# Even load of Q and K, reordered GpSimd, V tiles between projection tiles, norm in two halves, 18 groups of scores ahead of the loop

## The chip, the cores and the metric

One core of a Trainium2 chip runs the whole kernel. The metric is device time in microseconds, the median of the runs. Engine names: PE is TensorE, DVE VectorE, ACT ScalarE, POOL GpSimd, SP SyncE, which issues DMAs.

## The reference

Eight batches of 1024 tokens with 256 features go through one block: a layer norm, then two branches whose sum is added to the input. Branch one is sliding-window attention (16 heads of 16 features, blocks of 64 queries, each against three blocks of keys with a band) with output projection, residual, norm, a gelu MLP of 1024, residual, norm. Branch two sends each token through one of eight experts, chosen by the largest score.

```python
x = L0_attn_x
xn = _layernorm(x, axis=-1)
x = x + attn_block(xn, ...) + expert_block(xn, gate_w, expert_w)

# attn_block
q, k, v = (x @ Wq + bq), (x @ Wk + bk), (x @ Wv + bv)      # by block of W = 64 and head
scores = einsum('bnqhd,bnkhd->bhnqk', q, kc) * scale       # kc: three blocks of keys
scores = where(band & valid, scores, -1e9)
out = einsum('bhnqk,bnkhd->bnqhd', softmax(scores), vc)
a = out @ Wo + bo
h = layer_norm(a + x, g1, b1)
f = gelu(h @ W1 + c1) @ W2 + c2
return layer_norm(f + h, g2, b2)

# expert_block
chosen = argmax(einsum('bsh,eh->bse', x, gate_w))
return x + (x @ expert_w[chosen].T)
```

## The kernel before

Tokens lie in T = 8 tiles of 128; the heads form G = 4 groups of four. The kernel is software-pipelined over the batches: `turn(b)` exists once for each engine, and the engines meet only at semaphores (`Count` objects; `x.at(b, k)` is the k-th event of batch b). Each engine runs its own list strictly in the order of the code. A turn has four stages.

**The loop**, `for k in range(STEPS + LAG)`, STEPS = 32 (group g, tile t). TensorE makes the transposed scores of step k (`scores_t`), ScalarE their exponentials (`exps`), GpSimd cuts the band in two passes (`band`, L468 and L473; in steps 22 to 27, `SHARED`, VectorE has the second pass), and TensorE multiplies with V (`values`) two steps later. A softmax needs each row's maximum first: `scores` (L1208) makes the scores once more in the other layout, in the two banks `SB`, one for each parity of the heads, VectorE reduces them (`maxima`, L739), and after a group's eight tiles `max_cols` (L1223) transposes the maxima, again into `SB`; they go through DRAM (`max_rows_out`, `max_rows_in`) into a row of `q_s`. The scores run LEAD = 14 steps ahead of the transposed ones: 14 groups are made before the loop, 18 in it. Beside this the loop does the next batch's norm (`c1_tile`, `c1_stage`, GpSimd's `rstd` at step 8, `xn_tile` in steps 10 to 13), its transposes (steps 14 to 17) and its Q and K (`qk_third`, two thirds of a tile in each of steps 18 to 29). SyncE takes Q and K through DRAM (`pair_stores`, `stack_loads`).

**b_stage**: for each tile a transpose of the heads' outputs (L1287), `normalize`, a transpose (L1295), the product with Wo (L1303) in two banks, and `b_sum` with statistics for the norm. Then come `c2_stage`, V and gate scores of the next batch, and the norm: variance (L789), GpSimd's `rstd` (L409), `nm1_stage` (L793), ScalarE's `n1_tiles` (L946), four transposes.

**d_stage, first half**: sixteen units of W1 (`w1_unit`, six matmuls of 512 columns in two banks `TB`), gelu (L1031) and its split into high and low halves (L995, L820), with the next batch's routing (`one_hot`, `ranks`, `routing_...`) and six groups of scores after units 5, 7 to 15.

**d_stage, second half**: for each of eight tiles `w2_tile` (24 matmuls), the next batch's sorted tokens through their expert (two tiles of 15 each time: `sorted_transposes` L1148, `xs_high`, `xs_low` L736, `sorted_expert`, `y_out`), one group of scores, `f_stats` (L798) and `f_out`. VectorE waits before all of it for `h_rdy` and `res_y`, both from GpSimd (L837, L839).

GpSimd's list in a turn sets much of the order:

```python
for k in range(STEPS):
    band(b, k)                      # rstd of the next batch after k == T
residual(b + 1)                     # L480, L483
rstd(b, 1, ve1, rs1)
residual_attn(b + 1)                # L489
fetch(b, last)                      # gathers L521, then the add L527
send(b + 1)                         # scatters L507
residual_mlp(b)                     # L496, L499
for t in range(T): rstd(b, 2, ve2, rs2, t)
```

`fetch` waits until `store_res(b + 1)` has landed, since it writes into `x_sb`. `load_x` reads the batch after the next into `x_sb` late in the sorted tiles, and `send` scatters `xn` by expert.

## Time and profile before

| | us |
|---|---|
| median of 3 runs | 1473.32 |
| lowest and highest | 1461.51, 1473.76 |
| the profiled execution | 1471.13 |
| its span, first to last instruction | 1469.3 |
| PE busy in the span | 1200.0 (82%) |
| DVE, POOL, ACT busy | 924.3, 825.5, 726.5 |
| mean granted TensorE clock | 0.928 |

Matmuls are pipelined and their modelled ends overlap, so a busy PE is not PE at its peak; starts are the better measure. The page's chain of waits is followed back from the last instruction, at each step to what released it. In a timeline a row can merge several instructions of one line; the bracket at its end tells how long the engine was idle before it and what ended that.

### The profile page before, as it was taken

The numbers are of one execution on the slowest core, as the hardware profiler recorded it, in microseconds if no ns is written. First come the engines' busy times: TensorE is split into PE (matmuls) and PEld (weight loads), VectorE is DVE, ScalarE is ACT, GpSimd is POOL, SyncE is SP. The second block draws the span as 40 slices with busy tenths as digits, with TensorE's granted clock in tenths as the row PEclk, the third lists the DMA queues.
The fourth block names the chain that finished last, engine by engine and source line by source line (L and its number), as shares of the span: only waits on it lengthen the run. The fifth ranks groups of instructions, "written<-read, shape, count | busy, mean of one in ns | idle before, by whom it ended". The sixth has DMA issues, their size and how long they took to land.

```text
span 1469.3 us, 32444 instructions
## 1 busy us (share of the span) xinstructions
PE 1200.0 (82%) x11720; PEld 726.1 (49%) x11720; DVE 924.3 (63%) x2207; ACT 726.5 (49%) x1355; POOL 825.5 (56%) x1088
## 2 busy tenths in 40 slices
PE   0717898799879898898987898798986989878877
PEld 0414454554637445464545546374454645365445
DVE  8554657476656746776575766577474765656455
ACT  1304657146562574436572575526763365725661
POOL 6551568435781567625674457815676266834664
PEclk9958999899989899999998999898998999999989
DMA  8443081231723254230812327231532408122010
GB/s 250 120 130 116 31 199 50 80 127 44 163 76 104 73 132 99 72 125 31 199 51 80 126 59 156 69 109 67 147 85 72 124 32 202 54 85 87 3 29 29
DMA packets 93977, 142.89 MB, mean 97 GB/s; under 512 B 10592, under 2 KB 62688, under 8 KB 91744
## 3 DMA queue, kind: packets, MB, share of 16 engines
q1 hardware_dynamic: 87680, 124.04, 30.6%
q0 software_dynamic: 6144, 16.79, 3.6%
q8 instruction: 100, 1.64, 0.5%
q14 instruction: 53, 0.43, 0.1%
HBM read 74.47 MB, written 68.29 MB: 97 GB/s over the span
## 4 chain that ended last, share of the span: by engine, by line
PE 42%; POOL 26%; issue 12%; DVE 7%; ACT 3%; DMA 3%; another core or an unknown queue 0%; DVEq 0%; POOLq 0%; SPq 0%; ACTq 0%
PE bank L1180 6%; PE bank L1268 5%; PE bank L1078 5%; PE bank L1081 5%; PE bank L1079 5%; PE bank L1173 4%; POOL x_sb L521 4%; DVE m_sb L745 4%; POOL xs_dram L507 4%; POOL res_r L527 3%; POOL pool L496 3%; POOL pool L499 3%; POOL x_sb L483 3%; POOL x_sb L480 3%; PE bank L1148 2%
## 5 line engine op out<-in xcount | busy, mean ns | idle before, releaser
L981 ACT ACTIVATE pool<-bank 128x512 f32<-128x512 f32 x512 | 285.5, 596 | 150.9 <-PE bank L1180 147.5
L745 DVE TENSOR_REDUCE m_sb<-bank 128x2 f32<-128x384 f32 x512 | 261.5, 552 | 130.3 <-PE bank L1188 128.7
L468 POOL TENSOR_SCALAR_AFFINE_SELECT pool<-pool 128x512 f32<-128x512 f32 x256 | 183.6, 717 | 244.1 <-ACT pool L981 205.5
L1180 PE MATMUL bank<-q_s,k_s 128*128 128x256 f16 x1024 | 185.1, 289 | 15.7 <-ACT pool L981 8.8
L412 POOL TENSOR_TENSOR rs<-ve,neghalf 128x1 f32<-128x1 f32 x64 | 36.9, 577 | 251.7 <-DVE ve L806 251.7
L1268 PE MATMUL bank<-pool,v_a 128*32 128x256 f32 (+2 forms) x2560 | 166.7, 352 | 8.4 <-POOL pool L473 8.3
L970 ACT ACTIVATE xn<-bank 128x256 f32<-128x256 f32 x120 | 46.0, 384 | 224.4 <-PE bank L1081 218.6
L1173 PE MATMUL bank<-k_s,q_s 48*64 48x192 f16 x2048 | 99.1, 270 | 58.9 <-DVE m_sb L745 40.5
L1180 PEld LDWEIGHTS bank<-q_s,k_s 128*128 128x128 f16 x1024 | 82.5, 101 | 126.3 <-issue 97.4
L820 DVE TENSOR_TENSOR pool<-pool 128x512 f16<-128x512 f32 x128 | 105.5, 827 | 62.1 <-ACT pool L995 52.7
L473 POOL TENSOR_SCALAR_AFFINE_SELECT pool<-pool 128x512 f32<-128x512 f32 x208 | 133.4, 641 | 0.0
L1078 PE MATMUL bank<-w_h,pool 128*128 128x256 f16 x512 | 126.0, 288 | 0.5 <-DVE pool L798 0.5
L1079 PE MATMUL bank<-w_l,pool 128*128 128x256 f16 x512 | 125.6, 288 | 0.0
L1031 ACT ACTIVATE pool<-bank,c1c 128x512 f32<-128x512 f32 x128 | 87.7, 685 | 48.9 <-PE bank L1081 33.3
L1173 PEld LDWEIGHTS bank<-k_s,q_s 48*64 48x64 f16 x2048 | 42.4, 109 | 134.5 <-issue 134.5
L1078 PE MATMUL bank<-tr_h,w_h 128*128 128x512 f16 x256 | 98.9, 386 | 4.6 <-ACT pool L1031 4.4
L736 DVE TENSOR_TENSOR pool<-bank,pool 128x256 f16<-128x256 f32 x120 | 46.0, 417 | 85.8 <-POOL pool L499 61.9
L1079 PE MATMUL bank<-tr_l,w_h 128*128 128x512 f16 x256 | 98.5, 385 | 0.0
L1148 PE MATMUL bank<-ident,xn 128*128 128x128 f32 x240 | 46.8, 310 | 62.6 <-DMA xn<-xs_dram 59.7
L1268 PEld LDWEIGHTS bank<-pool,v_a 128*32 128x32 f32 x2560 | 53.5, 111 | 84.2 <-issue 45.4
L962 ACT ACTIVATE pool<-bank 128x256 f16<-128x256 f32 x120 | 41.3, 382 | 89.3 <-PE bank L1148 87.7
L995 ACT ACTIVATE pool<-pool 128x512 f16<-128x512 f32 x128 | 80.6, 630 | 4.1
(154 smaller groups left out, 2644.6 us busy)
## 6 DMA issues: line engine op xcount, KB each, us to landing
pair_dram<-pool SPq DMA_DIRECT2D x96, 256.0 KB, 4.2
xn<-xs_dram SPq DMA_DIRECT2D x40, 384.0 KB, 3.6
ys_dram<-xn SPq DMA_DIRECT2D x120, 128.0 KB, 1.8
q_s<-pair_dram SPq DMA_DIRECT2D x32, 384.0 KB, 6.7
k_s<-pair_dram SPq DMA_DIRECT2D x32, 384.0 KB, 8.3
x_sb<-in_L_attn_x SPq DMA_DIRECT2D x8, 1024.0 KB, 5.8
res_dram<-x_sb SPq DMA_DIRECT2D x8, 1024.0 KB, 5.2
res_r<-res_dram SPq DMA_DIRECT2D x8, 1024.0 KB, 5.0
```

The source lines that it names most:

```text
L468: nc.gpsimd.affine_select(out=p, in_=p, compare_op=ALU.is_ge, fill=0.0, base=0, pattern=[[0, 4], [1, 2 * W]], channel_multiplier=-1).then_ ...
L473: nc.gpsimd.affine_select(out=p, in_=p, compare_op=ALU.is_ge, fill=0.0, base=0, pattern=[[0, 4], [-1, 2 * W]], channel_multiplier=1).then_ ...
L745: nc.vector.tensor_reduce(m_sb[:, 4 * g + par:4 * g + 4:2, t], SB[par][:, 0:2 * WIN].rearrange("p (h c) -> p h c", h=2), AX.X, ALU.max).th ...
L820: nc.vector.tensor_tensor(gL[hf][:, c, :], g32[:, u % 2, :], gH[hf][:, c, :], ALU.subtract).then_inc(g_lo.sem, 1)
L981: nc.scalar.activation(prob[:, (k + 2) % 3, par::2, :], TB[par][:, :].rearrange("p (h q) -> p h q", h=2), ACT.Exp, scale=EXP_SCALE).then_i ...
L995: nc.scalar.activation(gH[hf][:, c, :], g32[:, u % 2, :], ACT.Copy).then_inc(g_hi.sem, 1)
L1031: nc.scalar.activation(g32[:, u % 2, :], TB[u % 2][:, :], ACT.Gelu_apprx_tanh, bias=c1c[:, c:c + 1], scale=1.0 / WS).then_inc(gel.sem, 1)
L1078: nc.tensor.matmul(dst, lh[c], rh[c], start=start and c == 0, stop=False)
L1079: nc.tensor.matmul(dst, lh[c], rl[c], start=False, stop=False)
L1173: return nc.tensor.matmul(out[W * n:W * n + W, i * WIN:i * WIN + WIN], q_s[r, 2 * h + par, q:q + W], k_s[r, h, q - W:q + 2 * W], start=i = ...
L1180: return nc.tensor.matmul(out[:, i * QW:i * QW + QW], k_s[:, h, W + t * P:W + t * P + P], q_s[:, 2 * h + par, t * P:t * P + QW], start=Tru ...
L1268: mm = nc.tensor.matmul(OB[hf][32 * hl:32 * hl + 32, a - hf * HALF:z - hf * HALF], v_a[:, t, 4 * g + hl, :], prob[:, (k + 2) % 3, hl, q0:q ...
```

## The change

- Loop: LEAD is 18, so 14 groups of scores are made in the loop (steps 1 to 14), one bank (parity) at a time between the transposed scores (`scores_half`). `xn_tile` moves to steps 2 to 5, the transposes to 6 to 9, Q and K are spread over steps 12 to 31 at 24 thirds in 20 steps (`thirds_at`). `max_cols` uses other banks (`XB`), for groups 0 and 1 in d_stage, 2 at step 10, 3 at step 16, and waits only for its own group's maxima.
- The next batch's `c1_tile` and `c1_stage` move from the loop to the second half of d_stage of the turn before, `load_x` from sorted tile 10 to tile 2; GpSimd's `rstd` for it stands ahead of the first `band`.
- GpSimd: the sixteen residual adds go between the bands of steps 6 to 21; the gathers go ahead of the second norm's root, which is made in two halves; the add of what was gathered is a step of its own (`add_fetched`). SyncE's `store_res` goes ahead of the last two stack loads.
- b_stage: V tiles of the next batch are made between the projection tiles, in the banks `SB`. `n1_stats`, `rstd_half`, `n1_shift` and `n1_tiles` work on four tiles each.
- d_stage: two more groups of scores, ahead of unit 0 and of unit 1, then one after each odd unit: ten ahead of the second half, eight in it. `one_hot` goes to b_stage, `ranks` behind unit 0, with the last two transposes of the norm.

The diff, cut to its core (SyncE, GpSimd, VectorE, ScalarE, TensorE in this order):

```diff
-LEAD = 14
-MAX_AT = 4
+LEAD = 18
+MAX_AT = {10: 2, 16: 3}
...
-    XN_AT = T + 2
...
-    QK_AT = XT_AT + 4
...
+    QK_AT = T + 4
+    RES_AT = XN_AT + 4
...
+    W1_STEPS = range(1, 2 * FC, 2)
+    assert 2 + len(W1_STEPS) + T == LEAD
...
+    def thirds_at(k):
+
+        n = STEPS - QK_AT
+        return range(max(0, k - QK_AT) * 24 // n, max(0, k + 1 - QK_AT) * 24 // n) if k < STEPS else range(0)
...
-        QB, VB = MB, OB + TB
+        QB, VB = MB, SB
+
+        XB = [MB[0], MB[1], MB[0], SB[1]]
...
-                    if i == 6:
+                    if i == 3:
                         max_rows_out(b, 0)
-                    if i == 8:
+                    if i == 5:
                         max_rows_in(b, 0)
-                    if i == 10 and x_next:
+                    if i == 2 and x_next:
                         load_x(b + 1)
...
+                    store_res(b + 1)
                     for i in range(2, 4):
                         stack_loads(b + 1, i)
-                    store_res(b + 1)
                     sorted_tiles(b + 1, x_next)
                 store_out(b)
...
+                if not last:
+                    rstd(b + 1, 0, ve0, rs0)
                 for k in range(STEPS):
                     band(b, k)
-                    if k == T and not last:
-                        rstd(b + 1, 0, ve0, rs0)
-                if not last:
-                    residual(b + 1)
-                rstd(b, 1, ve1, rs1)
+                    if RES_AT <= k < RES_AT + 2 * T and not last:
+                        residual_tile(b + 1, k - RES_AT)
+                fetch(b, last)
+                for hf in range(2):
+                    rstd_half(b, hf)
                 if not last:
                     residual_attn(b + 1)
-                fetch(b, last)
+                add_fetched(b)
                 if not last:
                     send(b + 1)
                 residual_mlp(b)
...
                         normalize(b, s)
+                        if not last:
+                            v_out(b + 1, s)
                     if s >= 4:
                         b_sum(b, s - 4)
-                dve.wait_ge(bn1.sem, bn1.at(b, T))
-                dve.sem_inc(passed, 1)
-                for t in range(T):
-                    nc.vector.bn_aggr(mv[:, 1, t, :], st[:, 1, t, :]).then_inc(ag1.sem, 1)
...
-                                               op0=ALU.mult, op1=ALU.mult).then_inc(nm1.sem, 1)
+                    if s == T - 1:
+                        n1_stats(b, 0)
+                n1_stats(b, 1)
+                n1_shift(b, 0)
+                if not last:
+                    one_hot(b + 1)
+                n1_shift(b, 1)
...
-                for u in range(0 if last else 2, 4):
+                for u in range(2):
                     n1_low(b, u)
                 if not last:
-                    one_hot(b + 1)
+                    maxima(b + 1, 0)
+                    routing_tiles(b + 1)
+                for u in range(2, 4):
+                    n1_low(b, u)
+                if not last:
+                    routing_positions(b + 1)
+                    maxima(b + 1, 1)
                 for u in range(2 * FC):
                     gelu_low(b, u)
                     if u == 0 and not last:
-                        routing_tiles(b + 1)
-                    if u == 1 and not last:
-                        routing_positions(b + 1)
-                    if u == 2 and not last:
                         routing_experts(b + 1)
                     if u in W1_STEPS and not last:
-                        maxima(b + 1, W1_STEPS.index(u))
+                        maxima(b + 1, 2 + W1_STEPS.index(u))
                 dve.wait_ge(res_y.sem, res_y.at(b, T))
...
                     if not last:
-                        if t == 3:
-                            max_cols(b + 1, 0)
+                        if t in (1, 7):
+                            max_cols(b + 1, t // 7)
                         maxima(b + 1, LEAD - T + t)
                     f_out(b, t)
+                    if t >= TH and b < NB - 2:
+                        for i in range(2 * (t - TH), 2 * (t - TH) + 2):
+                            c1_tile(b + 2, i)
                 if not last:
                     keep_positions(b + 1)
+                if b < NB - 2:
+                    c1_stage(b + 2)
...
+                        max_cols(b, MAX_AT[k])
                     if 1 <= k and k - 1 + LEAD < STEPS:
...
-                for u in range(4):
-                    hf, c = divmod(u, DC)
-                    act.wait_ge(nT_ps.sem, nT_ps.at(b, u + 1))
-                    nc.scalar.activation(tr_h[:, c, hf * HALF:hf * HALF + HALF], MB[u % 2][:, :], ACT.Copy).then_inc(nT_h.sem, 1)
+                n1_tiles(b, 0)
+                for u in range(2):
+                    n1_high(b, u)
+                n1_tiles(b, 1)
                 for u in range(2 * FC):
+                    if u == 1:
+                        for i in range(2, 4):
+                            n1_high(b, i)
                     c = u % FC
...
-                nc.tensor.transpose(SB[g % 2][0:4 * T, 0:P], m_sb[:, 4 * g:4 * g + 4, :].rearrange("p h t -> p (h t)"),
+            def scores_half(b, j, par):
+
+                scores_wait(b, j, par)
+                for i in range(2):
+                    for n in range(2):
+                        score_mm(SB[par], n, j, par, i)
+                for n in range(2):
+                    mm = mask_mm(SB[par], n, j % T, par)
+                mm.then_inc(S_ps.sem, 1)
+
+            def max_cols(b, g):
+                pe.wait_ge(mx.sem, mx.at(b, 2 * T * (g + 1)))
+                if g == 2 and b < NB - 1:
+                    pe.wait_ge(xT_l.sem, xT_l.at(b + 1, 3))
+                nc.tensor.transpose(XB[g][0:4 * T, 0:P], m_sb[:, 4 * g:4 * g + 4, :].rearrange("p h t -> p (h t)"),
                                     ident[:, :]).then_inc(mT_ps.sem, 1)
 
...
             def b_stage(b, last):
+                if not last:
+                    v_tile(b + 1, 0)
                 for s in range(T + 4):
                     if s < T:
...
                         mm.then_inc(t1_ps.sem, 1)
+                        if t + 1 < T and not last:
...
                     n1_transposes(b, u, last)
+                if not last:
+                    scores(b + 1, 0)
                 for u in range(2 * FC):
                     w1_unit(b, u, last)
-                    if u == 1 and not last:
-                        ranks(b + 1)
+                    if u == 0:
+                        if not last:
+                            ranks(b + 1)
+                        for i in range(2, 4):
+                            n1_transposes(b, i, last)
...
+                        if not last:
+                            scores(b + 1, 1)
                     if u in W1_STEPS and not last:
-                        scores(b + 1, W1_STEPS.index(u))
+                        scores(b + 1, 2 + W1_STEPS.index(u))
...
                 for k in range(STEPS + LAG):
-                    if k % T == MAX_AT and k < 3 * T:
-                        max_cols(b, k // T + 1, min(k - 1 + LEAD, STEPS))
+                    if k in MAX_AT:
+                        max_cols(b, MAX_AT[k])
                     for par in range(2):
                         if k < STEPS:
                             scores_t(b, k, par)
-                        if QK_AT <= k < QK_AT + 12 and not last:
-                            qk_third(b + 1, *divmod(2 * (k - QK_AT) + par, 3))
-                    if 1 <= k and k - 1 + LEAD < STEPS:
-                        scores(b, k - 1 + LEAD)
+                        if not last:
+                            for third in list(thirds_at(k))[par:par + 1]:
+                                qk_third(b + 1, *divmod(third, 3))
+                        if 1 <= k and k - 1 + LEAD < STEPS:
+                            scores_half(b, k - 1 + LEAD, 1 - par)
```

## Rows read from the trace of the kernel before

**Rows 1.** The page: chain of waits by engine; a DMA issue, with median us to landing
```profile
PE 42%; POOL 26%; issue 12%; DVE 7%; ACT 3%; DMA 3%; another core or an unknown queue 0%; DVEq 0%; POOLq 0%; SPq 0%; ACTq 0%
...
res_dram<-x_sb SPq DMA_DIRECT2D x8, 1024.0 KB, 5.2
```
**Rows 2.** Windows: start:end, length, busy us by engine, clock, DMA share, GB/s
```profile
481.10:549.20 68.10, 60.95 (x733) 28.62 (x734) 40.45 (x88) 47.21 (x85) 40.80 (x62) 0.92 0.36 101
549.20:564.20 15.00, 14.08 (x94) 11.96 (x93) 12.66 (x42) 3.61 (x9) 10.32 (x15) 1.00 0.84 204
...
614.00:651.90 37.90, 37.05 (x393) 30.31 (x390) 28.15 (x76) 10.41 (x30) 4.64 (x9) 1.00 0.33 106
```
**Rows 3.** Timeline, GpSimd, 548 to 615: start, us, engine, line, operation
```profile
548.44 5.53 POOL L480 TENSOR_TENSOR x_sb<-x_sb,xn 128x256 f32<-128x256 f32 x8
...
564.31 1.65 POOL L409 TENSOR_TENSOR rs<-ve,neghalf 128x8 f32<-128x8 f32 x1 [4.72 <-DVE ve L789]
...
571.61 1.06 POOL L521 DMA_INDIRECT x_sb<-ys_dram,pos_y  x1 [0.16 <-issue]
...
583.39 7.41 POOL L527 TENSOR_TENSOR res_r<-res_r,x_sb 128x256 f32<-128x256 f32 x8 [1.90 <-DMA x_sb<-ys_dram,pos_y]
...
607.23 7.18 POOL L499 TENSOR_TENSOR pool<-pool,bc 128x256 f32<-128x256 f32 x8
```
**Rows 4.** Waits: who waited for whom, us in total, times, longest
```profile
DVE pool L736 <- POOL pool L499: 61.9, 7, 12.4
```
**Rows 5.** Timeline, TensorE: first matmuls of two V tiles
```profile
562.71 0.29 PE L1078 MATMUL bank<-wvg_h,tr_h 128*128 128x264 f16 x1 [0.52 <-DVE pool L772]
...
563.39 0.28 PE L1078 MATMUL bank<-wvg_h,tr_h 128*128 128x264 f16 x1
```
**Rows 6.** Timeline, VectorE: a V tile's evacuation, and one step's maxima
```profile
564.14 0.42 DVE L666 SCALAR_TENSOR_TENSOR v_a<-bank,bc 128x256 f32<-128x256 f32 x1
...
1362.15 1.02 DVE L745 TENSOR_REDUCE m_sb<-bank 128x2 f32<-128x384 f32 x2 [0.77 <-PE bank L1188]
```
**Rows 7.** Timeline, ScalarE: the norm's tiles and the load of gelu's table
```profile
566.72 4.04 ACT L946 ACTIVATE pool<-pool,nm,rs 128x256 f32<-128x256 f32 x8 [5.78 <-DVE nm L793]
...
574.76 1.28 ACT L1031 ACT_TABLE_LOAD   x1
```
**Rows 8.** Timeline, ScalarE: a stop in one turn; first and last gelu of another
```profile
582.95 0.69 ACT L1031 ACTIVATE pool<-bank,c1c 128x512 f32<-128x512 f32 x1 [4.31 <-remote]
...
916.92 0.69 ACT L1031 ACTIVATE pool<-bank,c1c 128x512 f32<-128x512 f32 x1
...
941.29 0.67 ACT L1031 ACTIVATE pool<-bank,c1c 128x512 f32<-128x512 f32 x1
```
**Rows 9.** Timeline, TensorE, one loop step with transposes (the next begins at 517.59)
```profile
515.49 0.61 PE L1180 MATMUL bank<-q_s,k_s 128*128 128x256 f16 x4
516.03 0.36 PE L1173 MATMUL bank<-k_s,q_s 48*64 48x192 f16 x8
...
516.44 0.66 PE L1087 MATMUL bank<-ident,xn 128*128 128x128 f32 x4
...
517.02 0.64 PE L1268 MATMUL bank<-pool,v_a 128*32 128x256 f32 x8
```
**Rows 10.** Timeline, TensorE, last turn: scores of two steps in a row
```profile
1361.53 0.36 PE L1173 MATMUL bank<-k_s,q_s 48*64 48x192 f16 x8 [0.21 <-DVE m_sb L745]
...
1363.32 0.36 PE L1173 MATMUL bank<-k_s,q_s 48*64 48x192 f16 x8 [0.20 <-DVE m_sb L745]
```
**Rows 11.** Timeline, TensorE: scores before and after a transpose of maxima
```profile
488.36 0.53 PE L1173 MATMUL bank<-k_s,q_s 48*64 48x192 f16 x8
...
491.35 0.36 PE L1173 MATMUL bank<-k_s,q_s 48*64 48x192 f16 x8
```
**Rows 12.** Timeline, last turn: GpSimd's last band pass, VectorE's first `f_stats`
```profile
1389.50 0.64 POOL L473 TENSOR_SCALAR_AFFINE_SELECT pool<-pool 128x512 f32<-128x512 f32 x1
...
1443.20 0.42 DVE L798 SCALAR_TENSOR_TENSOR pool<-bank,pool 128x256 f32<-128x256 f32 x1 [2.79 <-POOL pool L499]
```

185 lines of the change are left out of this document (94 added, 91 removed).

## The prediction

> **What bounds the kernel now.** I read the page first: its chain of waits says whether one engine sets the end. None does; TensorE has 42% of the chain, GpSimd 26%, and 12% is waiting that nothing explains [rows 1]. The windows of one turn of the batch loop, cut at the table loads that start the exponentials (481.1 and 651.9), show where to look: the turn takes 170.8 us, the attention loop 68.1 of them, the output projection 15.0 with TensorE busy for 14.1, and the second half of the feed-forward part 37.9 with TensorE busy for 37.05 [rows 2]. Only in the 50 us between, from 564 to 614, is TensorE loose. GpSimd's timeline says what runs there [rows 3]: the residual adds start when the loop ends (548.44) and end at 559.59 (564.31 less its 4.72 of waiting); then the reciprocal root; the bias add, 5.6 us; eight gathers from 571.61; the add of what they brought, 7.4 us to 590.8; eight scatters; two passes over `n1`, to 614.4. The scatters take 10.9: 607.23 less 590.8 less a first pass that I take at 5.5, like the equal residual pass. VectorE's waits close it: `xs_low` waited for L499, the last pass, in all seven turns, 61.9 us [rows 4]. So GpSimd's queue is the path from the loop's end (549.1) to 614.4, 65.3 us of each 170.8.
>
> **GpSimd's queue after the change.** Removed from it behind the loop are the 11.1 us of residual adds. Moved are the gathers, ahead of the root, so that they run beside the output projection; what is queued behind their waits is the root itself. They wait for `store_res`, which stands in SyncE's queue behind the pair stores of the last Q/K tile: 1 us after the loop's end plus 5.2 us to land [rows 1], in a crowded stretch, so I take 8 (bounds 4 and 15). With 11 us for issue and landing (571.61 to 583.39 less a 1.90 us wait is 9.9) they end 19 after the loop. Then two half roots, 1.0 each (estimate from 1.65 for all eight columns), 5.6, 7.4, 10.9 and 12.8: 56.7 us in place of 65.3. Alone this would be worth 8.6 us a turn.
>
> **The other path becomes the later one.** TensorE, ScalarE and VectorE have their own chain from the loop's end to the first `f_stats`.
> - Output projection. A V tile costs 0.68 us of TensorE (562.71 to 563.39) [rows 5]; eight are 5.4. They leave a stretch where they lay under the norm's chain for one where TensorE is full (14.1 of 15.0). Some 1 us fits into its first gaps, and half of the statistics are done early (0.4): 15.0 + 5.4 - 1.4 = 19.0. VectorE gets 8 x 0.42 [rows 6] on its 12.7: 16.1, just below. Bounds: 18 (gaps of 2) and 22 (the two engines in turn).
> - Norm. Four tiles 2.0 (half of 4.04), first transposes 0.9, two copies 1.1 (estimate, a little over a tile of 0.5 each), four tiles 2.0, table 1.3 [rows 7]: 7.4; and 0.8 for the shift, since the root stands behind the gathers. First gelu at 19.0 + 8.2 = 27.2 after the loop. Before it was 576.05 - 549.1 = 27.0: the V tiles eat what the halves give.
> - Sixteen gelus. First to last start took 24.4 us in a quiet turn; in another ScalarE stood for 4.31 us at an unknown queue and it was 33 [rows 8]. I take 27.0 for the mean. Two more groups of scores are in it, 0.55 each (0.40 of TensorE, 516.03 to 516.44 [rows 9], and a hand-over). VectorE's order at the start is new: two `n1_low`, maxima, five routing operations, two more `n1_low`, four more of routing, maxima, and only then `gelu_low(0)`, for which the third gelu waits. That is some 5.5 us (1.0 for each maxima [rows 6], 0.7 for a pass of 512 columns, 0.25 for the small ones, estimates) against 2.6 for two gelus: 3 us late, two copies of ScalarE hidden in it. 27.0 + 1.1 + 3.0 = 31.1; bounds 26 and 36.
> - Last gelu to first `f_stats`: 0.7, transposes 0.5, `w2_tile` 24 matmuls or four V tiles, 2.7: 3.9.
>
> That is 62.2 us after the loop. Before it was 614.4 and one pass of 0.4 for `xs_low`, so 65.7 to 66. GpSimd's 56.7 now ends before. Gain 3.7, bounds -1 and 8.
>
> **The loop.** A step with transposes takes 2.10 us, all TensorE's: 0.54 for the transposed scores, 0.40 for scores and masks, 0.59 for transposes, the rest 0.57 for values [rows 9]. A plain step has 1.51 of such work but takes 1.79 (1361.53 to 1363.32), for both score banks are filled together and VectorE must empty them before the next [rows 10]. One bank at a time takes that wait away, but the score matmuls then run two abreast and not four. The 0.40 us now hold four streams of 640 columns. Two abreast, each half costs those 640 columns (0.27 us at 2.4 GHz) and about 0.1 for the change of tile shape (516.03 less 515.49 less 4 x 0.107): 0.75 a step. Bounds: 0.53, no cost for the change, and 1.17, nothing abreast. I take 0.75, as the interval with four abreast holds that same 0.1.
> The Trainium skill, TensorEngine Tiling (Array Packing), Key Properties, says that changing the tiling mode drains the engine; the row agrees, with some 0.1 us. The change goes from three such changes in a scoring step to five, so by that rule the halves are not free; by a free change of mode a step would cost 0.2 less.
>
> Step by step after: 2.5 to the first band and 1.2, as now; step 1 2.4; 2 to 5 VectorE's, maxima 1.02 and two tiles of `xn`, 2.1; 6 to 9 1.86 + 0.59 = 2.45; 10 and 11 2.0; 12 to 14 with a third of a Q/K tile (0.43) 2.3; 15 to 21 GpSimd's, two bands of 0.62 and one residual tile 0.69 [rows 3, 12], 1.93; 22 to 30 0.57 + 0.54 + 1.2 x 0.43 = 1.65; 1.8 from the last band to the last values. Sum 65.4. The transposes of the maxima are in it at nothing: three of them stopped the scores for 1.2 us each, 2.99 from 488.36 to 491.35 in place of 1.79 [rows 11]; now they use the banks of the `xn` transposes and scores long finished, and if they collide there it costs 0.3 each. The root for the next batch now stands ahead of the first band, behind `c1_stage` at the end of VectorE's turn: 0.6 late. So 66.0 for 68.0: 2.0 gained, bounds -4 (halves at 1.17) and 6.
>
> **The second half.** TensorE sets it (37.05 of 37.9 [rows 2]). The stop for the maxima's transpose goes there too, 0.8 (like the 1.2 in the loop, less for the tile beside it). Eight `bn_stats` of 0.42, a pass of 256 columns as in [rows 6], go into the last four tiles, 0.84 each, where VectorE, busy for 28.15 of the 37.9, has 1.2 idle in each, half of it usable. I take 1.2 lost: 0.4 worse, bounds -0.8 and 3. `load_x` in the middle of the sorted loads: 0.6, bounds 0 and 2.
>
> **The sum.** 3.7 + 2.0 - 0.4 - 0.6 = 4.7 us a turn, seven turns: 33. The last turn has no V, no Q/K and no scatters: its loop loses four scoring steps and two stops, 3.6, and its first `f_stats` comes at 48 in place of 53 us after the loop (1443.2 less the last band's end, 1390.1 [rows 12]), 5.2. The prologue gains four groups of scores, beside GpSimd's sends, and 4 us of statistics partly in the way: 2.5 lost. 33 + 8.8 - 2.5 = 39.3. The profiled execution took 1471.1: 1431.8, and the median of the runs shown is 2.2 above it: 1434.
>
> **The rivals.**
> 1. *As forecast*, the gate moves from GpSimd to the chain through the gelus, 2.5 to 7 us a turn: 1418 to 1452. Chance 0.52.
> 2. *More*: VectorE keeps pace at the start of the gelus (26 to 28 us in all) and the halves cost 0.53: 4 us more a turn: 1385 to 1418. For it speaks that TensorE has slack there, against it the fixed order. Chance 0.24.
> 3. *Taken back in the loop*: halves at 1.17, 14 x 0.42 = 5.9 us a turn less than forecast: 1434 + 41 = 1475; 1460 to 1478. Against it: L1268 runs its column groups abreast in one bank, eight matmuls of 256 columns in 0.57 [rows 9]. Chance 0.11.
> 4. *It does not do what it says*: the gathers get free only 15 us after the loop, the queue ends at 64, and nothing is gained there: 1455 to 1470. Chance 0.04.
> 5. *Slower*: stops of ScalarE for an unknown queue [rows 8]. Before, they lay ahead of GpSimd's gate and cost nothing; now each one counts. The place is between the first and the last gelu; at 37 us in each turn (6 more than I take) the time is 1476, and it decides from 39: 1490. One turn had 33 with two groups fewer. Chance 0.09.
>
> **How the numbers follow.** The runs shown differ by 0.8%, so about 1% can be told: below 1458.6 is faster, above 1488 slower. Faster: 1 and 2, 0.76. Same: 3 and 4, 0.15. Slower: 0.09. Range: from 1405, which cuts a third of case 2, to 1466, within cases 3 and 4.
>
> **What would show it.** Right: no wait of `xs_low` for L499; the gathers inside an output projection of 19 us; scoring steps of 1.9 us; no stop at the maxima's transposes. Wrong: an output projection above 22 us, first to last gelu above 34, a loop above 68.

## The result, and the profile after

The kernel after takes 1557.18 us (median of 4 runs, 1546.97 to 1590.88), the one before 1473.54 in the same session: ratio 1.055, interval 1.047 to 1.063. It is slower by 5.5%, and the forecast was 1434. Ratios with an interval, here and below, are of the executions in the faster of two states that every kernel shows; where "no interval" is said, too few were in it, and the ratio is the rougher one of the medians of all. The profiled execution has a span of 1555.6 us, 123.8 more than the 1431.8 of the forecast's sum.

The page of the kernel after: span, granted clock of TensorE in 40 slices (tenths of full speed), chain of waits by engine, and the group of the gathers (busy, mean ns | idle before it, and what ended it).

```profile
span 1555.6 us, 32461 instructions
...
PEclk9957699979898598977989699995889889896799
...
PE 68%; DVE 14%; issue 7%; ACT 5%; DMA 3%; POOL 2%; SPq 0%; DVEq 0%; POOLq 0%; ACTq 0%
...
L541 POOL DMA_INDIRECT x_sb<-ys_dram,pos_y x64 | 61.4, 960 | 77.7 <-DMA res_dram<-x_sb 60.5
```

GpSimd's share of the chain fell from 26% [rows 1] to 2%: the gate has moved, as forecast. But TensorE's went from 42% to 68%. The windows of the turn that begins at 494.4 say where (columns as in [rows 2]: PE, PEld, DVE, ACT, POOL busy, clock, DMA share, GB/s).

```profile
494.40:499.40 5.00, 3.44 (x28) 1.62 (x28) 4.42 (x18) 4.13 (x6) 1.12 (x1) 0.80 0.51 176
499.40:529.40 30.00, 29.64 (x214) 12.14 (x216) 15.58 (x28) 11.35 (x20) 14.73 (x24) 0.50 0.15 51
529.40:549.40 20.00, 20.00 (x188) 8.16 (x180) 8.11 (x15) 11.38 (x20) 13.13 (x22) 0.78 0.01 3
549.40:577.00 27.60, 24.87 (x262) 11.44 (x261) 11.71 (x13) 21.96 (x41) 20.74 (x31) 1.00 0.61 144
577.00:598.60 21.60, 18.36 (x128) 15.24 (x126) 15.79 (x60) 3.69 (x10) 8.77 (x10) 1.00 0.89 208
```

The loop takes 82.6 us here (494.4 to 577.0) against 68.1 before [rows 2]. For 30 us TensorE is busy 29.64 us by the trace, whose ends of matmuls are modelled, and is granted 0.50, that is 1.2 GHz. The output projection, 21.6, runs at full clock. In the timeline of TensorE one scoring step at 1.2 GHz looks like this (start, us, line; L1222 transposed scores, L1215 and L1230 a half's scores and masks, L1129 transposes of `xn`, L1319 values):

```profile
521.24 0.61 PE L1222 MATMUL bank<-q_s,k_s 128*128 128x256 f16 x2
521.77 0.53 PE L1215 MATMUL bank<-k_s,q_s 48*64 48x192 f16 x4
522.10 0.42 PE L1230 MATMUL bank<-mask,ident 64*64 64x256 bf16 x2
522.45 0.61 PE L1222 MATMUL bank<-q_s,k_s 128*128 128x256 f16 x2
522.99 0.53 PE L1215 MATMUL bank<-k_s,q_s 48*64 48x192 f16 x4
523.31 0.42 PE L1230 MATMUL bank<-mask,ident 64*64 64x256 bf16 x2
523.66 1.11 PE L1129 MATMUL bank<-ident,xn 128*128 128x128 f32 x4
524.70 1.08 PE L1319 MATMUL bank<-pool,v_a 128*32 128x256 f32 x8
525.72 0.61 PE L1222 MATMUL bank<-q_s,k_s 128*128 128x256 f16 x2
```

The step is 4.48 us long (521.24 to 525.72) against 2.10 before [rows 9], and nothing in it waits: no row has an idle time. From start to start transposes and values have almost doubled, 1.04 for 0.58 and 1.02 for 0.57; the transposed scores with the halves take 2.42 for 0.95. What changed is the clock.

The turns of the kernel after differ among themselves, and their loops are the longer the lower the clock was. These are the whole loops of the turns from 1046.0 and from 320.7, the longest and the shortest of the seven full ones:

```profile
1046.00:1130.50 84.50, 80.40 (x687) 33.95 (x684) 39.85 (x73) 48.75 (x85) 49.57 (x75) 0.72 0.28 77
320.70:393.10 72.40, 68.73 (x683) 30.53 (x684) 39.72 (x73) 48.74 (x84) 49.71 (x75) 0.86 0.34 89
```

The code is the same in both, and so are the busy times of VectorE, ScalarE and GpSimd (columns three to five).

Stages, means over the seven full turns, read from the timelines as distances between first and last instructions (for the kernel before the same reading). "Loop" runs from the table load of the exponentials to the last values, "first to last gelu" from the first one's start to the last one's end (the forecast's 31.1 was from start to start; 0.7 for the last gelu is added here and taken from its 3.9 behind):

| us | before | forecast | after |
|---|---|---|---|
| loop | 68.3 | 66.0 | 79.3 (72.4 to 84.5) |
| loop of the last turn | 56.3 | 52.7 | 73.6 |
| output projection | 14.8 | 19.0 | 21.3 |
| loop's end to first gelu | 26.1 | 27.2 | 29.7 |
| first to last gelu | 27.1 | 31.8 | 31.3 (28.7 to 35.0) |
| loop's end to first `f_stats` | 65.1 | 62.2 | 64.2 |
| first `f_stats` to the turn's end | | 38.3 | 38.0 |

Against the forecast: 7 x 13.3 = 93 us in the loops of the full turns, 73.6 - 52.7 = 21 in the last one, 7 x 2.0 = 14 between loop and `f_stats`. That is 128, less 1 in the last turn and 2 in the second halves: 125 for the 124 us of the miss. Nine tenths of it are in the loop.

### The profile page after: what moved, and what is told of

Its sections match the earlier page's. It is cut to its first block, busy times and chain, and to the rows that moved or that the text cites. A ratio compares the mean times of both kernels' runs of the same rounds, so it can differ in the third digit from the quotient of the medians.

```text
span 1555.6 us, 32461 instructions
## 1 busy us (share of the span) xinstructions
PE 1349.9 (87%) x11720; PEld 764.7 (49%) x11720; DVE 975.9 (63%) x2223; ACT 741.3 (48%) x1355; POOL 817.1 (53%) x1096
## 3 DMA queue, kind: packets, MB, share of 16 engines
q8 instruction: 100, 1.64, 0.4%
## 4 chain that ended last, share of the span: by engine, by line
PE 68%; DVE 14%; issue 7%; ACT 5%; DMA 3%; POOL 2%; SPq 0%; DVEq 0%; POOLq 0%; ACTq 0%
PE bank L1222 10%; PE bank L1319 10%; PE bank L1120 9%; PE bank L1121 8%; PE bank L1123 8%; PE bank L1215 7%; PE bank L1129 3%; PE bank L1230 3%; DMA ys_dram<-xn 2%; PE bank L1190 2%; DVE st L634 2%; PE bank L1358 2%; DVE xn L663 2%; PE bank L1154 2%; DVE pool L775 2%
## 5 line engine op out<-in xcount | busy, mean ns | idle before, releaser
L1022 ACT ACTIVATE pool<-bank 128x512 f32<-128x512 f32 x512 | 299.7, 599 | 214.6 <-PE bank L1222 210.5
L1222 PE MATMUL bank<-q_s,k_s 128*128 128x256 f16 x1024 | 230.8, 316 | 12.7 <-ACT pool L1022 8.8
L1215 PE MATMUL bank<-k_s,q_s 48*64 48x192 f16 x2048 | 161.5, 297 | 55.9 <-DVE m_sb L763 45.2
L1319 PE MATMUL bank<-pool,v_a 128*32 128x256 f32 (+2 forms) x2560 | 187.5, 391 | 18.3 <-POOL pool L486 9.8
L1222 PEld LDWEIGHTS bank<-q_s,k_s 128*128 128x128 f16 x1024 | 74.1, 102 | 174.2 <-issue 143.1
L1215 PEld LDWEIGHTS bank<-k_s,q_s 48*64 48x64 f16 x2048 | 60.6, 117 | 185.2 <-issue 185.2
L852 DVE TENSOR_TENSOR pool<-pool 128x512 f16<-128x512 f32 x128 | 117.7, 922 | 47.0 <-ACT pool L1036 45.9
L1230 PE MATMUL bank<-mask,ident 64*64 64x256 bf16 x1024 | 129.1, 329 | 0.0
L682 DVE SCALAR_TENSOR_TENSOR pool<-bank,bqk,pool 128x512 f16<-128x512 f32 x64 | 47.9, 749 | 113.8 <-ACT pool L998 112.8
L1120 PE MATMUL bank<-w_h,pool 128*128 128x256 f16 x512 | 115.3, 273 | 0.0
L1319 PEld LDWEIGHTS bank<-pool,v_a 128*32 128x32 f32 x2560 | 58.9, 119 | 94.2 <-issue 42.4
L541 POOL DMA_INDIRECT x_sb<-ys_dram,pos_y x64 | 61.4, 960 | 77.7 <-DMA res_dram<-x_sb 60.5
```

What stands on the lines that cost most here:

```text
L852: nc.vector.tensor_tensor(gL[hf][:, c, :], g32[:, u % 2, :], gH[hf][:, c, :], ALU.subtract).then_inc(g_lo.sem, 1)
L1022: nc.scalar.activation(prob[:, (k + 2) % 3, par::2, :], TB[par][:, :].rearrange("p (h q) -> p h q", h=2), ACT.Exp, scale=EXP_SCALE).then_i ...
L1120: nc.tensor.matmul(dst, lh[c], rh[c], start=start and c == 0, stop=False)
L1215: return nc.tensor.matmul(out[W * n:W * n + W, i * WIN:i * WIN + WIN], q_s[r, 2 * h + par, q:q + W], k_s[r, h, q - W:q + 2 * W], start=i = ...
L1222: return nc.tensor.matmul(out[:, i * QW:i * QW + QW], k_s[:, h, W + t * P:W + t * P + P], q_s[:, 2 * h + par, t * P:t * P + QW], start=Tru ...
L1230: return nc.tensor.matmul(dst, ident16[r, :], band, start=False, stop=True, skip_group_check=True)
```

## The experiments

Kernels sent together ran on one chip, one after the other, beside the kernel before; ratios are to that. There were five such groups, A to E. Why they have to be kept apart comes out in C and D.

| group | before, us | kernels |
|---|---|---|
| A | 1480.07 | a_full, b_half, a_adj, a_twice |
| B | 1483.84 | a_v1, a_late_fetch, a_between, n_latev |
| C | 1475.88 | a_warm, a_cold, n_shift, n_split |
| D | 1486.38 | after_2, a_adj_2, a_warm_2, n_early |
| E | 1471.03 | n_shift_2, n_safe |

### Is it the halved scores?

**a_full**: scores four abreast again, behind both transposed scores; all else of the change stays.

```diff
-                        if 1 <= k and k - 1 + LEAD < STEPS:
-                            scores_half(b, k - 1 + LEAD, 1 - par)
+                    if 1 <= k and k - 1 + LEAD < STEPS:
+                        scores(b, k - 1 + LEAD)
```

> The changed kernel with one thing undone: in the loop's 14 scoring steps both parities of a group are made together, four score matmuls abreast, behind the two transposed scores, as before the change. Theory CLOCK (the score matmuls two abreast keep TensorE at its lower level of 1.2 GHz until the scores are done): granted clock back to 0.92 or more, loop 66 to 69 us instead of 72 to 85, 1435 to 1455 us in all. Rival PLACE (the low clock comes from what the change put into the loop's first steps, norm, transposes, and the later start of Q and K): the loop stays above 76 us and the time above 1500.

Measured: 1468.61 us, ratio 0.993 (0.989 to 0.996), mean clock 0.94 against 0.87; loop 62.6. The clock came back as the theory said, the loop was shorter than its 66 to 69, and the time, outside its 1435 to 1455, was longer for another reason (the section on 1466 and 1436). One edit of the change carries the loss: 6% against the 1.055 of the kernel after, 7 to 10% against its repeat in group D (1575.90 to 1622.06 us there).

**b_half**: the other side. The kernel before, with only its scores halved and interleaved in the same way (the diff above reversed, with `scores_half` added).

> The kernel before with this one part of the change: scores made one parity at a time, each behind its transposed score, in the 18 scoring steps of the loop. Theory CLOCK: granted clock near 0.85, steps of 3.4 us at the lower level, loop 80 us or more, 1560 to 1620 us. Rival PLACE: the halves cost only their work at full clock, 0.75 for 0.40 us of which the old wait for VectorE hides most: 1480 to 1500 us.

Measured: 1668.09 us, ratio 1.120 (1.111 to 1.129), mean clock 0.81, full turns' loops of 82 to 96 us. The halves alone do it, and without the rest of the change they do it worse than the expected 1560 to 1620. The shortest of these loops, from 926.6, is worth a look:

```profile
928.60:952.50 23.90, 22.05 (x278) 9.76 (x280) 18.08 (x48) 14.93 (x26) 16.27 (x25) 1.00 0.26 89
952.50:983.00 30.50, 30.43 (x207) 12.38 (x208) 12.45 (x22) 11.90 (x21) 8.57 (x14) 0.50 0.01 2
```

Here the first eleven steps with halves ran at full clock. The clock fell at 952.5, after TensorE had waited 0.91 and 0.45 us around a transpose of maxima, and stayed at 0.50 until the scoring steps were over.

**a_adj**: still two halves, each with its own wait and bank, but one behind the other, after both transposed scores.

```diff
-                        if 1 <= k and k - 1 + LEAD < STEPS:
-                            scores_half(b, k - 1 + LEAD, 1 - par)
+                    if 1 <= k and k - 1 + LEAD < STEPS:
+                        scores_half(b, k - 1 + LEAD, 1)
+                        scores_half(b, k - 1 + LEAD, 0)
```

> The changed kernel, with the two halves of a group one right behind the other, behind both transposed scores: still two abreast, but changes of tile shape as few as before the change. Theory CLOCK by streams abreast: nothing is cured, 1530 to 1560 us, scoring steps of 3.2 to 3.4 us at 1.2 GHz. Rival SHAPES (it is the alternation of transposed scores and halves that holds the clock down): 1440 to 1470 us.

Measured: 1466.28 us, ratio 0.993 (0.989 to 0.997), loop 62.8, clock 0.94. The halves may stay, if they are adjacent, and the expectation named for that case is the one met. My theory, that two streams abreast in place of four keep the clock down, does not fall with it, though the expectation said so: as the step below shows, adjacent halves overlap and do run four abreast. Its windows for the turn from 482.2, and one of its steps with transposes:

```profile
487.20:492.20 5.00, 3.80 (x38) 1.37 (x38) 3.19 (x7) 1.08 (x2) 4.71 (x8) 0.51 0.33 96
492.20:517.20 25.00, 25.00 (x346) 13.13 (x342) 17.92 (x37) 18.44 (x34) 21.25 (x35) 0.96 0.11 43
```

```profile
500.84 0.61 PE L1222 MATMUL bank<-q_s,k_s 128*128 128x256 f16 x4
501.38 0.37 PE L1215 MATMUL bank<-k_s,q_s 48*64 48x192 f16 x8
501.57 0.29 PE L1230 MATMUL bank<-mask,ident 64*64 64x256 bf16 x4
501.80 0.66 PE L1129 MATMUL bank<-ident,xn 128*128 128x128 f32 x4
502.38 0.64 PE L1319 MATMUL bank<-pool,v_a 128*32 128x256 f32 x8
502.95 0.61 PE L1222 MATMUL bank<-q_s,k_s 128*128 128x256 f16 x4
```

The clock falls to 0.51 at the loop's start in this kernel too, and comes back within the next window; in the kernel after it stays down for 30 us. The step takes 2.11 us. The two adjacent halves take 0.42 together (501.38 to 501.80), as four abreast did [rows 9]: issued back to back they lie on different rows of the array and overlap. Set apart, they take 0.39 each even at full clock: in the kernel after, one runs from 543.16 to the next transposed score at 543.56, 0.40.

```profile
543.16 0.35 PE L1215 MATMUL bank<-k_s,q_s 48*64 48x192 f16 x4
543.35 0.28 PE L1230 MATMUL bank<-mask,ident 64*64 64x256 bf16 x2
543.56 0.39 PE L1222 MATMUL bank<-q_s,k_s 128*128 128x256 f16 x2
```

**a_between**: whole scores, but between the two transposed scores of a step: four changes of tile shape in a step, where the kernel after has five and a_adj three.

```diff
-                        if 1 <= k and k - 1 + LEAD < STEPS:
-                            scores_half(b, k - 1 + LEAD, 1 - par)
+                        if par == 0 and 1 <= k and k - 1 + LEAD < STEPS:
+                            scores(b, k - 1 + LEAD)
```

> The kernel after with its scores four abreast again but placed whole between the two transposed scores of a step: TensorE changes between full-array and quarter-array tiles four times in a scoring step, against five with the halves interleaved and three with the scores behind both transposed scores. If the cost is in the number of changes, the loop falls between the two: 63 us with three changes, 72 to 84 with five, so 66 to 74, and the total about 1480 to 1530. If what counts is that a score lies between the two transposed scores at all, it is as slow as the kernel after, 1540 to 1570. If it is the halves alone, it is as the version with whole scores behind, 1465 to 1472.

Measured: 1478.45 us, ratio 1.000 (0.996 to 1.004), loop 64.2 (63.6 to 65.1), clock 0.94, below the 66 to 74 and the 1480 that were expected of four changes. One more change of shape costs 1.4 us a loop and leaves the clock alone. The kernel after, 15 us more, differs from it in two things at once: five changes for four, and score matmuls that run two abreast and not four. No run has one without the other, so which of the two holds the clock down is not shown. What is shown is that halves set apart by a full-array matmul do it, and whole scores or adjacent halves do not.

**a_twice**: the kernel after with each transposed score of the scoring steps made twice, the same result written again. It adds only work.

```diff
-                for i in range(2):
-                    mm = score_t_mm(TB[par], k, par, i)
+                for r in range(2 if 1 <= k <= STEPS - LEAD else 1):
+                    for i in range(2):
+                        mm = score_t_mm(TB[par], k, par, i)
```

> The changed kernel with work added: in the 14 scoring steps each transposed score is made twice, the second time over the first with the same values, four more matmuls of the full array a step. At 1.2 GHz that is 0.85 us more a step, at 2.4 GHz 0.43. Theory CLOCK, if what counts is how much of the array's work there is: the clock rises earlier, and the kernel gets faster by the added work, 1470 to 1530 us. If the added matmuls do not bring the clock up: 14 x 8 x 0.85 = 95 us slower, 1640 to 1660 us.

Measured: 1538.16 us, ratio 1.046 (1.037 to 1.055; the kernel after 1.047 to 1.063), mean clock 0.95, loop 71.7; 1470 to 1530 was expected. It has 14 x 4 matmuls of 256 columns more in a turn, 6 us at the 0.107 of the forecast, and its loop is 7.6 us shorter than that of the kernel after (79.3; 81.0 in group D). Its clock hardly falls: in four of the seven full loops not at all, in the others for 3 to 7 us. One without a fall, from 502.4:

```profile
502.40:517.40 15.00, 12.69 (x148) 6.85 (x148) 12.37 (x34) 8.29 (x13) 8.45 (x12) 1.00 0.45 156
517.40:537.40 20.00, 20.00 (x227) 10.79 (x225) 11.55 (x21) 11.62 (x20) 12.97 (x22) 1.00 0.01 3
```

More work in the loop, less time for it: the loss is in the clock and not in the work. In a_twice interleaved halves do not hold the clock down.

### Does interleaving pull the clock down, or does it keep it from coming back?

**a_warm**: adjacent halves in the first seven scoring steps (k 1 to 7), interleaved ones in the other seven (k 8 to 14). **a_cold**: the reverse.

```diff
 # a_warm
-                        if 1 <= k and k - 1 + LEAD < STEPS:
+                        if 8 <= k and k - 1 + LEAD < STEPS:
                             scores_half(b, k - 1 + LEAD, 1 - par)
+                    if 1 <= k < 8:
+                        for par in range(2):
+                            scores_half(b, k - 1 + LEAD, 1 - par)
```

> The kernel after with its half scores adjacent, behind both transposed scores, in the first seven scoring steps of a turn (k from 1 to 7), and interleaved as in the kernel after in the other seven (k from 8 to 14). In every kernel so far the granted clock falls to about 0.5 in the first 10 us of the loop; with adjacent halves it is 1.00 again 10 to 15 us after the loop began, with interleaved ones it stays at 0.50 for 35 us with TensorE busy throughout. If interleaving only hinders the clock's return once it is down, it is up by step 8 and stays up: the loop takes 62 to 65 us and the kernel 1460 to 1480 us. If interleaving takes the clock down by itself, the granted clock falls to 0.5 to 0.7 from step 8 on, at about 20 us into the loop, and the kernel takes 1500 to 1530 us.

> The reverse: interleaved halves in k from 1 to 7, adjacent ones from 8 to 14. If interleaving hinders the clock's return, the clock stays at 0.5 until step 8, at 27 to 30 us into the loop (7 steps of 3.4 us), and comes back within a few steps of it, so the loop takes about 7 x 1.5 = 10 us more than with adjacent halves: 70 to 74 us, the kernel 1510 to 1540. If it takes the clock down by itself in later steps only, the kernel is near 1466 us.

Measured: a_warm 1436.55 us, ratio 0.976 (0.969 to 0.984), loop 65.9; a_cold 1486.74, ratio 1.008 (1.003 to 1.012), loop 71.0. The loops are 0.9 above and within what the theory of the return gave (62 to 65 and 70 to 74); both times are 23 us below its ranges, which were reckoned from a_adj's 1466 and so held something that this group does not have (next section). Windows of a_warm (turn from 471.4), then of a_cold (turn from 483.4):

```profile
476.40:481.40 5.00, 3.89 (x40) 1.44 (x37) 3.01 (x7) 1.30 (x3) 4.71 (x8) 0.50 0.38 100
481.40:491.40 10.00, 10.00 (x136) 5.05 (x134) 8.23 (x18) 6.52 (x12) 6.63 (x12) 0.85 0.25 101
491.40:496.40 5.00, 5.00 (x58) 2.52 (x57) 3.66 (x8) 3.42 (x6) 3.96 (x7) 1.00 0.01 2
496.40:511.40 15.00, 15.00 (x175) 6.85 (x177) 7.40 (x14) 10.61 (x19) 12.72 (x21) 1.00 0.01 3
```

```profile
488.40:508.40 20.00, 19.16 (x149) 7.58 (x148) 11.29 (x21) 7.35 (x13) 9.86 (x17) 0.50 0.22 76
508.40:513.40 5.00, 5.00 (x41) 2.41 (x41) 2.27 (x4) 2.57 (x5) 3.10 (x6) 0.60 0.01 2
513.40:528.40 15.00, 15.00 (x204) 7.57 (x203) 8.64 (x17) 11.73 (x22) 13.89 (x24) 1.00 0.01 3
```

In a_warm the interleaved steps begin at 496 and run at 1.00, here and in all its turns. In a_cold's turn the clock stays at 0.50 as long as the steps are interleaved; the first adjacent one begins at 510.25 and the next, at 513.29, is at full speed. So interleaving does not take the clock down; once it is down, it delays its return. How long is not fixed. In two of a_cold's seven full turns the clock was back during the last interleaved step, and in the kernel after it comes back with the steps still interleaved in all seven: in steps 7 to 9 in three turns, in step 12 in three, in step 14 in one, after 20 to 48 us. From step 6 on transposes of the full array join, from step 12 on matmuls of Q and K. In the turn of the windows the return falls on the first of these (two matmuls of 512 columns, then a half at full speed):

```profile
537.25 0.63 PE L1154 MATMUL bank<-tr_h,wqk_h 128*128 128x512 f16 x1
...
538.24 0.39 PE L1215 MATMUL bank<-k_s,q_s 48*64 48x192 f16 x4
```

In a_twice, too, more full-array work stands beside the halves. Whether that or the order decides, the runs do not separate.

A fall near the head of the loop occurs in every version, though not in every turn, in the kernel before too (0.57 and 0.74 in its windows from 483.3 to 493.3), and what goes before it is TensorE's waiting there: 3.44 us busy in the first 5 of the kernel after.

a_warm is the kernel after but for seven steps of each turn, and measured 1436.6 where 1434 was forecast. Its other stages are those of the kernel after: projection 21.4, loop's end to `f_stats` 62.6. This close a figure is luck in part: its seven adjacent steps save 2.6 us a turn (group D), 18 in all, which the forecast kernel would not have.

### Why adjacent halves gave 1466 and not 1436

In group A the loop of a_adj was 62.8 us, shorter than forecast, and still the gain was 0.7%. The loss was behind the loop: projection 26.1, first `f_stats` 69.4 after the loop's end, forecast 19.0 and 62.2. Five runs asked what is in that.

**a_v1**: a_adj with only the first of the six matmuls of each V tile of batches 1 to 7 (the V rows and gates of those batches are therefore others, and the routing with them).

```diff
-                mm = triple(VB[t % 2][:, 0:D + E], ...)
+                mm = nc.tensor.matmul(VB[t % 2][:, 0:D + E], tr_h[:, 0, s], wvg_h[:, 0], start=True, stop=True)
```

> The kernel after with its two half scores adjacent, and of each V tile of batches 1 to 7 only the first of its six matmuls of width 400 made (the other five left out, so V and the gates of those batches are not the reference's). The question is the output projection, which took 25.6 us from the end of the loop to the first V eviction in the parent, where the prediction had 19. If the matmuls of V are what lengthens it, 8 x 5 fewer matmuls at 0.17 to 0.33 us each give 7 to 13 us per turn less of TensorE's work, and the stretch falls to about 16 to 20 us; the time falls by 7 turns x 6 to 9 us, from 1466 to about 1400 to 1425 us. If it is the chain through the extra tile's eviction and semaphores, or the stops that the trace lays on an unknown queue, the stretch stays at 23 to 26 us and the time above 1450.

Measured: 1451.38 us, ratio 0.980 (0.972 to 0.988); projection 23.4. Forty matmuls fewer gave 2.7 us (across groups A and B). They have 264 columns, not the 400 of the expectation, so what was left out is 5/6 of 8 x 0.68 [rows 5], 4.5 us and not 7 to 13: the matmuls are a part of it, the stops or the evictions the rest.

**a_late_fetch**: a_adj with the gathers back behind the roots and the bias add, out of the projection.

```diff
-                fetch(b, last)
                 for hf in range(2):
                     rstd_half(b, hf)
                 if not last:
                     residual_attn(b + 1)
+                fetch(b, last)
```

> The kernel after with adjacent halves and the row gathers put back behind the roots and the residual on GpSimd, so that no gather runs inside the output projection. If the gathers' traffic (DMA engines busy 0.78 in that stretch) is what stops VectorE and ScalarE there, the stretch falls from 25.6 to about 19 to 21 us, and the gathers then gate the feed-forward again: the first gelu at 35 us or later, total 1455 to 1475. If V's work is what lengthens it, the stretch stays at 24 to 26 us, and the total rises by the later gathers, to 1475 to 1500.

Measured: 1491.71 us, ratio 1.006 (1.003 to 1.009); projection 21.4, just above the 19 to 21 of the first theory, but first to last gelu 37.2 where a_adj had 31.8. The total was missed, since the lost time went along with the gathers: what had stopped the projection now stopped the gelus. After the loop's end a_adj issues its gathers at 7.9 to 17.7 us, and stops end at 16 to 20; here it is 28.3 to 38.4 and 35 to 40. A second set goes with GpSimd's scatters: issued at 39 to 51 us and stops ending at 45 to 53 in a_adj, 47 to 58 and 54 to 60 here.

What stopped them is marked in the timelines as ended by "remote", another core or an unknown queue. In the kernel after no such instruction exists, in a_warm and a_cold neither; a_adj, a_full, a_twice, a_v1, a_between and a_late_fetch have 29 to 40 of them, n_latev (below) 13, the kernel before 8, b_half 6. **after_2**, **a_adj_2** and **a_warm_2** are the kernel after, a_adj and a_warm again, together.

> The kernel after once more, beside the others of this call. Expected as before: the loop 72 to 85 us at a granted clock of 0.5 in its first 35 us, no stop that the trace lays on an unknown queue, 1545 to 1570 us.

> The kernel after with adjacent halves once more. In its first profile VectorE and ScalarE stood still together in each output projection for 2 to 5.6 us, ended by something of another core or an unknown queue, while the gathers ran; in the kernels of the last call, with the same projection and the same gathers beside it, no such stop is in any turn. If the stops come with the chip or the hour, they are absent here too, the projection takes 21.3 us instead of 25.6, and the time is about 4.3 x 7 = 30 us below 1466: 1430 to 1440 us. If they belong to this kernel's code, they are here again and the time is 1455 to 1475.

> The kernel with adjacent halves in its first seven scoring steps and interleaved ones behind, once more. If the stops come with the chip or the hour, it measures the same as the version with adjacent halves throughout, or up to 15 us more (its loop was 65.7 us against 62.8). If they belong to the other kernel's code, it is 25 to 35 us faster.

Measured in group D: after_2 1609.45 us (1575.90 to 1622.06; 1.083 of the kernel before by the medians, no interval), a_adj_2 1470.82, ratio 0.989 (0.985 to 0.993), a_warm_2 1500.82, ratio 1.009 (1.004 to 1.013). Projections 26.8, 26.8, 26.5. All three have the stops, a_warm_2 too, which had none in group C and 0.976. So whether there are any does not belong to the code: in A, B and D every kernel traced shows them, in C and E none. Nor does it belong to the chip: A and E ran on the same one. Where and how long they are does depend on the code: n_latev, in group B with the same early gathers but no V tiles there, has none in the projections of its seven full turns. After_2's expectation, no stops, was wrong.

Two of them in a_adj_2, ScalarE's row first, then VectorE's:

```profile
563.67 0.38 ACT L1057 ACTIVATE pool<-bank 128x256 f32<-128x256 f32 x1 [5.82 <-remote]
```

```profile
563.61 0.42 DVE L790 TENSOR_TENSOR pool<-bank,xnbo 128x256 f32<-128x256 f32 x1 [1.91 <-remote]
...
565.08 0.26 DVE L781 RECIPROCAL rec<-bank 128x16 f32<-128x16 f32 x1 [0.58 <-remote]
```

Both engines come back at the same moment, 563.6, in a stretch where the DMA engines are 0.74 busy, and TensorE's clock is 0.87 over the projection (its window in a_adj_2, then in a_warm of group C):

```profile
546.10:572.00 25.90, 21.04 (x125) 16.49 (x122) 14.55 (x51) 3.15 (x9) 8.75 (x9) 0.87 0.74 171
```

```profile
537.00:560.00 23.00, 19.58 (x148) 15.65 (x140) 16.13 (x57) 4.56 (x11) 9.94 (x11) 1.00 0.85 195
```

That they follow the gathers, and the scatters, is shown (a_late_fetch moved both). What they are is not. A candidate is the engines' own instructions arriving late: the page of the profile has a queue "q8 instruction" with 100 packets and 1.64 MB, the same in the runs without stops. The Trainium skill, Runtime: NRT & Kernel Launch, Instruction fetch mechanics, says that each engine's instructions are fetched by DMA in blocks of 16 KiB; the page of the profile agrees in size, 16.4 KB a packet. No run shows that these packets come late, nor why some groups have stops and others not.

Inside group D a_warm_2 is 2% slower than a_adj_2, with loops of 65.5 and 62.9. The loops are 18 us of the 30 between the medians; the traces, of executions of 1485.0 and 1468.89 us, do not show the rest. Seven interleaved steps at full clock cost 2.6 us, 0.37 each, which is the 2 x 0.39 of two halves apart less the 0.42 of two together.

### A version from the findings

**n_latev**: whole scores behind the transposed ones; V tiles out of the projection, four before the norm's first transposes, two behind them, two behind the first W1 unit; 16 groups of scores ahead in place of 18.

```diff
             def d_stage(b, last):
+                if not last:
+                    for t in range(TH):
+                        v_tile(b + 1, t)
                 for u in range(2):
                     n1_transposes(b, u, last)
-                if not last:
-                    scores(b + 1, 0)
+                if not last:
+                    for t in range(TH, TH + 2):
+                        v_tile(b + 1, t)
...
```

> A version of my own: scores whole and behind both transposed scores, V tiles taken out of the output projection and put around the norm's first transposes (four before, two behind, two after the first projection unit), sixteen groups of scores ahead, GpSimd's early gathers kept. If TensorE's work in the output projection is what the kernel after loses there, the projection returns to 15 to 17 us after the loop's end, the V tiles fill the wait for the norm, the first gelu comes at 27 to 30 us, and the time is 1396 to 1430. If the stops there are the gathers' traffic, the projection stays above 20 us and the time is 1440 to 1465.

Measured: 1457.20 us (1438.32 to 1466.52; 0.982 by the medians, no interval). The projection is at 15.0 again, as expected, the total was missed by 27 us at the median and by 8 at the lowest. In three turns the first gelu comes 7 us later than in the rest, and one row of VectorE says why, beside GpSimd's:

```profile
398.25 8.31 DVE L807 SCALAR_TENSOR_TENSOR nm<-mv,rs 128x4 f32<-128x4 f32 x1
406.48 0.41 DVE L687 SCALAR_TENSOR_TENSOR v_a<-bank,bc 128x256 f32<-128x256 f32 x1
```

```profile
401.06 5.47 POOL L549 TENSOR_TENSOR res_r<-res_r,x_sb 128x256 f32<-128x256 f32 x8
```

The norm's shift has 4 elements in a partition and takes 0.15 us elsewhere. Here it came in the midst of sixteen back-to-back sums of GpSimd and lasted until the last had ended, 406.53. In three turns it lasted 8.0 to 8.3; in the other four full turns it came as far into the same sums (2.6 to 3.0 us) and took 0.2 to 0.5.

**n_shift**: both shifts together, after the V evictions. **n_split**: also the roots behind the first four gathers instead of behind all eight. The edit of n_shift against n_latev:

```diff
 # n_shift
                 n1_stats(b, 1)
-                n1_shift(b, 0)
                 if not last:
                     for t in range(TH):
                         v_out(b + 1, t)
+                n1_shift(b, 0)
                 n1_shift(b, 1)
```

> The version with V tiles around the norm, with VectorE's norm shift of the second half put straight behind that of the first. In the parent the second shift, 0.16 us of work on SBUF operands, took 8.31 us in three of the eight turns (398.25 to 406.56, until GpSimd's row of sixteen residual sums ended at 406.53), and 0.5 us in the others. If GpSimd's sums shut it out when it comes in the midst of them, and it comes ahead of them now, those three turns lose 8 us each and the time falls from 1457 to 1425 to 1440 us. If the 8 us are something else, the long shift stays and the time is 1445 to 1465.

> The version before this one, with GpSimd's roots of the norm behind the first four gathers instead of behind all eight. In the parent the roots are ready about 3.5 us after the variances, since GpSimd still issues gathers (1.25 us each). If that wait stands on the path, each of 8 turns gains about 3 us: 24 us less than the version before this one, 1400 to 1415 us. If the projection's own end or the gathers' traffic comes last, the gain is below 8 us.

Measured: n_shift 1427.66 us, ratio 0.967 (0.962 to 0.972); its longest shift is 0.71 us. n_split 1432.28, ratio 0.971 (0.965 to 0.976), 1400 to 1415 expected. The shift's stop is gone, but group C has none of the other stops either, so the 30 us between n_latev and n_shift are not all the shift's: three times 7 to 8 are 21 to 24. n_split brought the first gelu 2.4 us forward (26.0 for 28.4 after the loop's end) and gave it back between first and last gelu (33.8 for 29.7): no gain. GpSimd's queue is near the path again there; n_shift's waits have it:

```profile
POOL xs_dram L527 <- DVE pos L738: 45.4, 7, 7.8
...
DVE pool L754 <- POOL pool L519: 15.1, 6, 2.5
```

**n_early**: n_shift with seven V tiles ahead of the norm's transposes, and ranks and positions earlier, so that the scatters start earlier.

```diff
                     if u == 0:
...
                         for i in range(2, 4):
                             n1_transposes(b, i, last)
-                    if u == 1 and not last:
-                        ranks(b + 1)
+                        if not last:
+                            ranks(b + 1)
...
```

> The version with the V tiles around the norm and both shifts together, with seven of the V tiles ahead of the norm's first transposes and the ranks behind the first projection unit instead of the second, so that the scattered rows' positions are ready earlier. In the parent GpSimd stood still for 6.3 us before the scatters, waiting for the positions, and VectorE waited 2.5 us for GpSimd's last sum at the first f_stats. If GpSimd's queue sets the first f_stats there, each of 7 turns gains about 2 to 3 us: 1427 less 15 to 20 us, 1405 to 1415. If TensorE does, nothing is gained: 1422 to 1432.

Measured: 1493.24 us, ratio 0.997 (0.992 to 1.002), in group D; neither expectation came. Its first gelu comes 38.5 after the loop's end in the trace (of an execution of 1496.44 us, above the median), 10 later than n_shift's. The shifts stand behind five V evictions where n_shift has four; a stop of 1.3 us and more holds these up, the shifts miss the gap before GpSimd's sums, and six of them last 7.4 to 7.5 us. Whether its earlier scatters are worth anything can't be read from this.

**n_shift_2** and **n_safe**: n_shift again, and with both shifts ahead of the four V evictions.

> The version with V tiles around the norm and both shifts together once more. It measured 0.967 of the kernel before in a call in which no trace had stops by an unknown queue. If there are none again: 0.960 to 0.972. If there are, they hold VectorE up in its V evictions, its shifts then fall into GpSimd's row of sums and last 8 us, and it measures 0.98 to 1.00.

> The same with both shifts ahead of the four V evictions on VectorE, so that nothing that can be late stands between the roots and the shifts. The evictions come about 4 us later, and TensorE waits for them with the third V tile, so without stops it is 0 to 3 us per turn slower than the other (0.967 to 0.985). If stops are there and the shifts' place is what they hurt, no shift lasts over 1 us here, and it is 15 to 40 us faster than the other.

Measured: 1424.80 us, ratio 0.969 (0.966 to 0.971), and 1427.27, ratio 0.969 (0.966 to 0.972). Neither has a stop, so what they were to tell apart, how each stands up to the stops, is left open. What they do show is that the gain of n_shift repeats: 3.1 to 3.3% faster than the kernel before in two sessions, on two chips.

## Why the prediction was wrong

- **The step that failed** is the sum "step by step after" of the loop, 65.4 us. It costs every step at the durations of [rows 9], which were read at full clock, though [rows 2] gave 0.92 for the loop. At full clock its terms nearly hold: a half 0.39 to 0.40, so 0.78 a step for the 0.75 taken. But a step had no term for the clock, and the change altered how long the clock stays down: at the head of the loop 7 to 10 us in six of the seven full turns before, 20 to 48 us after. The loops came out 13.3 us a turn above the forecast and 21 in the last. Most of it is the clock: with the clock as a_adj had it the loop would be some 68 us, an estimate from a_adj_2's 62.9 and twice the 2.6 us that seven interleaved steps cost in a_warm_2, so 11 of the 13.3 are the clock's and 2 the sum's.
- **The rivals** were three sizes of the same sum and one of ScalarE's stops. Rival 3, "taken back in the loop", had the right place and 5.9 us a turn where 13.3 went, since its price (1.17 for halves with nothing abreast) was again one at full clock. In the prediction's own words the drain at a change of shape was worth 0.1 us, a direct price that the 0.39 of a half bears out; what halves set apart cost by way of the clock had no term and no rival.
- **GpSimd's gate moved** (26% to 2% of the chain), no wait of `xs_low` for the last pass is left, and the gathers start 7.8 us after the loop's end (90.4 - 82.6 in the turn of the windows) where 8 was taken. Right. Rival 4 fell. The queue's terms (19, 2.0, 5.6, 7.4, 10.9, 12.8) add up to 57.7 and not to the 56.7 written, and it ended at 57.5 to 61.0; both are ahead of the other path, so nothing hangs on it.
- **Output projection**: 21.3 for 19.0, inside the bounds of 18 to 22, near the end where the engines take turns. The term that was too small is the V tile in the chain: 6.5 us for eight (21.3 - 14.8) against 4.0 net. TensorE's busy time in the stretch went from 14.08 [rows 2] to 18.36, 4.3 us more. Some 2.3 are idle time more, 1.1 of it TensorE waiting for a V tile's eviction on VectorE (0.42 and a copy, between two normalizations); the rest is not resolved.
- **Norm, gelus, first `f_stats`**: first gelu at 29.7 for 27.2 (2.3 of it the projection), then 31.3 for 31.8 and 3.1 for 3.2; together 64.2 for 62.2. In four of seven turns it was 61.9 and in three 67. In the three a pass of 0.69 us on VectorE took 5.1 to 5.6 (below). The 31.8 was thus near as a mean by luck: in a quiet turn it is 28.8. Its 3 us for VectorE's order rest on a sum of 5.5 whose terms (four passes of 0.7, two maxima of 1.0, nine small ones of 0.25) add up to 7.
- **Rival 5**, a stop between the gelus that decides, did not decide here. Stops for an unknown queue are real, and in groups A, B and D they cost the changed kernels 26.1 - 21.4 = 5 us in the projection and 7 us up to `f_stats`; the kernel before differs by 0.3 to 1.0% between the groups. In the run that was forecast there were none.
- **What would have given it away**: the loop's 0.92 in [rows 2], and windows of 5 us, which show the kernel before at 0.57 early in its loop. A change that puts smaller tiles and more changes of shape exactly there should have had a rival with the scoring steps at half clock: twice [rows 9] and [rows 10] is about 2 us more a step, and for seven of the fourteen steps 14 us a turn, some 1530 us (an estimate made afterwards).

## What to carry to other kernels

Cost TensorE's steps at the clock they will run at, and look where the granted clock dips before you put small tiles, shape changes or gaps there. Keep matmuls on parts of the array together; two halves issued back to back cost 0.42 us where they cost 0.78 apart, and apart they can hold the clock down. A VectorE operation on SBUF alone that can fall into a long run of GpSimd's should be placed ahead of it by order, and not left to timing. Compare only kernels that ran together: one and the same kernel was at 0.976 and at 1.009 of its reference in two sessions.

## What the runs showed of the hardware

- **The clock can stay at half while TensorE is busy.** 29.64 of 30.00 us busy at 0.50, for 20 to 48 us in a turn; with more full-array work (a_twice) it hardly falls, and with the same work in another order (a_adj) it is back after 7 to 10 us. The Trainium skill, TensorE: Matmul & The Clock Gate, Part 1, ties the full clock to how busy TensorE has lately been. By the busy time of the trace this case does not agree. What makes the difference is open: the kernel after (79.3 us of loop) has five changes of shape in a step and its score matmuls two abreast, a_between (64.2) four changes and four abreast.
- **GpSimd's run shuts VectorE out.** In the kernel after, turn from 677.7, GpSimd's first pass over `n1` and VectorE's `gelu_low`:

```profile
804.34 5.48 POOL L516 TENSOR_TENSOR pool<-pool,bc 128x256 f32<-128x256 f32 x8
809.90 6.74 POOL L519 TENSOR_TENSOR pool<-pool,bc 128x256 f32<-128x256 f32 x8
```

```profile
803.49 0.69 DVE L852 TENSOR_TENSOR pool<-pool 128x512 f16<-128x512 f32 x1 [0.34 <-ACT pool L1036]
804.79 5.59 DVE L852 TENSOR_TENSOR pool<-pool 128x512 f16<-128x512 f32 x1 [0.60 <-ACT pool L1036]
810.30 1.01 DVE L763 TENSOR_REDUCE m_sb<-bank 128x2 f32<-128x384 f32 x2
```

  The pass took 5.59 instead of 0.69 and ended at 810.38, 0.56 us after GpSimd's first run (809.82); the first instruction of the second run took 1.05 instead of 0.72. It did not get in between two of the eight instructions of the first run. The Trainium skill, SBUF — State Buffer, SBUF: two separate sides, calls the port pair of the two engines an exclusive lock for the whole instruction; the rows agree that it is exclusive, but here it kept VectorE out over eight instructions of GpSimd, 0.72 us each, and over the rest of sixteen in n_latev (8.31 us). Since other passes got in midway, what decides is open.
- **VectorE and ScalarE stop while GpSimd's gathers and scatters are in flight**, for up to 7 us and often until the same moment, in some sessions and not in others on the same chip. The cause is open.
